# Moving loads, queue entries and three bias additions in a one-launch decoder layer: three phases in one program on one core

## What is computed

```
x = layernorm(x + attn(x))            # 16 heads, "quantum" scores; softmax of s/s
x = layernorm(x + xattn(x, ctx))      # two softmaxes per head, gain 0.3, norm per head, output matmul
x = layernorm(x + ffn(x))             # router picks 2 of 4 experts per token

# ffn, per token, with weights rw of the two chosen experts
e0 = silu(x @ sw_w1) * (x @ sw_w3) @ sw_w2
e1 = gelu(sym @ me_c1w + b) @ me_c2w + me_c2b
e2 = layernorm(h2 + ff) @ ce_gen_w + ce_gen_b
e3 = gelu(x @ ml_w1 + b) @ ml_w2 + ml_b2
out = sum over the chosen experts of rw * e
```

## Time and profile before

| | |
|---|---|
| median of 3 runs | 1595.86 us (1591.67 to 1597.58) |
| profiled execution, its time / its span | 1598.66 us / 1596.9 us |
| busy: PE, PEld, DVE, ACT, POOL | 95%, 68%, 72%, 53%, 23% |
| chain that ended last | PE 86%, DVE 6%, ACT 2%, issue 2%, SPq 2%, DMA 1% |
| mean granted TensorE clock | 0.97 of full |
| transfers issued by SP | 95.41 MB in all; ST 256 x 96 KB, KT 128 x 192 KB, QT 128 x 96 KB |

### The profile page before, as it was taken

The page is one execution under the profiler, slowest core; times in us unless marked ns, Lnnn a source line. Parts: engine busy times, 40 slices in busy tenths (PEclk is TensorE's granted clock), DMA queues, the critical chain, the costliest instruction groups (busy, mean ns, idle before and its releaser), DMA issues.

```text
span 1596.9 us, 28806 instructions
## 1 busy us (share of the span) xinstructions
PE 1523.8 (95%) x11272; PEld 1079.7 (68%) x11272; DVE 1141.8 (72%) x2311; ACT 847.4 (53%) x1121; POOL 367.8 (23%) x399
## 2 busy tenths in 40 slices
PE   6999999888799999999999899999999999999998
PEld 3334333334466666666657788898989888888887
DVE  5445555456699999999964787767676777777675
ACT  4888889763588888888873232222222122222221
POOL 0000100121446666666451320000000000000000
PEclk9999999886799999999998999999999999999999
DMA  7755556355467575665652100000000000000000
GB/s 144 137 108 109 109 109 135 60 87 96 62 95 112 76 111 92 103 96 81 100 166 67 47 14 1 14 1 14 1 14 1 14 1 14 1 1 14 1 14 14
DMA packets 61574, 97.23 MB, mean 61 GB/s; under 512 B 12588, under 2 KB 29880, under 8 KB 61440
## 3 DMA queue, kind: packets, MB, share of 16 engines
q1 hardware_dynamic: 61440, 95.41, 32.9%
HBM read 26.16 MB, written 4.19 MB: 19 GB/s over the span
## 4 chain that ended last, share of the span: by engine, by line
PE 86%; DVE 6%; ACT 2%; issue 2%; SPq 2%; DMA 1%; POOL 0%; POOLq 0%; DVEq 0%; ACTq 0%
PE ps L109 82%; PE ps L1128 2%; SPq L119 2%; ACT PX L1282 1%; ACT H L536 1%; DVE EE L658 1%; PE ps L1090 1%; PE ps L1136 1%; DVE XC L1937 1%; DVE NM L1337 0%; PE ps L1745 0%; PE ps L1060 0%; DMA TA<-TX 0%; PE ps L1736 0%; DVE XH L571 0%
## 5 line engine op out<-in xcount | busy, mean ns | idle before, releaser
L1337 DVE TENSOR_REDUCE NM<-ps 128x4 f32<-128x1024 f32 x256 | 307.8, 1221 | 46.5 <-PE ps L109 45.1
L1282 ACT ACTIVATE PX<-ps 128x1024 f32<-128x1024 f32 x256 | 262.4, 1025 | 82.0 <-PE ps L109 81.0
L536 ACT ACTIVATE H<-ps,b1c 128x1024 f32<-128x1024 f32 x256 | 268.6, 1118 | 43.4 <-PE ps L109 41.8
L1897 ACT ACTIVATE GF<-ps,cols 128x512 f32<-128x512 f32 x128 | 88.2, 689 | 300.9 <-PE ps L109 300.8
L109 PE MATMUL ps<-XC,W_sw_w 128*128 128x512 f32 x768 | 187.3, 395 | 0.0
L2088 DVE CAST GH<-GF 128x512 fp32r<-128x512 f32 x192 | 82.1, 428 | 112.1 <-ACT GF L1897 107.1
L109 PEld LDWEIGHTS ps<-XC,W_sw_w 128*128 128x128 f32 x768 | 141.6, 190 | 28.3
L2196 POOL TENSOR_SCALAR RSc<-AGc 128x4 f32<-128x4 f32 x23 | 6.9, 301 | 607.5 <-DVE AGc L1983 607.5
L109 PE MATMUL ps<-PX,VT 128*32 128x256 f32 x2048 | 141.4, 395 | 1.6 <-DVE X L583 1.5
L1892 ACT ACTIVATE GF<-ps 128x512 f32<-128x512 f32 x64 | 38.2, 597 | 189.0 <-PE ps L109 189.0
L109 PE MATMUL ps<-KT,QT 48*128 48x512 f32 x512 | 132.8, 518 | 5.4 <-DVE NM L1337 3.0
(11 more groups left out here) (233 smaller groups left out, 2567.9 us busy)
## 6 DMA issues: line engine op xcount, KB each, us to landing
ST<-QS SPq DMA_DIRECT2D x256, 96.0 KB, 2.8
KT<-KS SPq DMA_DIRECT2D x128, 192.0 KB, 4.7
QT<-XSb SPq DMA_DIRECT2D x128, 96.0 KB, 4.1
XT<-in_xT_dram SPq DMA_DIRECT2D x8, 512.0 KB, 4.0
raw_a<-in_x_dram SPq DMA_DIRECT2D x8, 512.0 KB, 4.3
CR<-in_ctxT_dram SPq DMA_DIRECT2D x8, 512.0 KB, 5.8
out_dram<-X SPq DMA_DIRECT2D x7, 512.0 KB, 3.0
R_sw_w<-in_sw_w_dram SPq DMA_DIRECT2D x6, 512.0 KB, 5.4
```

The lines of the kernel that those rows point to most:

```text
L536: e.activation(H1[s % 8][:, :, :], PP[s % 3][:, :, :], ACT.Tanh, bias=b1c[:, half:half + 1], scale=1.0).then_inc(act_th, 1)
L1282: e.activation(PX[s % 3][:, :, :, :], PP[2][:, :, :].rearrange("p g (c q) -> p g c q", c=2), ACT.Exp, bias=0.0, scale=0.25).then_inc(act_e ...
L1337: e.tensor_reduce(NM[u % 2][:, qc, :, :, i], PP[qc][:, :, :].rearrange("p g (m k) -> p g m k", m=2), AX.X, ALU.max, negate=True).then_inc( ...
L1897: e.activation(g[:, :], o, f, bias=cols[:, col:col + 1], scale=1.0).then_inc(act_g, 1)
```

## The change

1. SP's `first()` is cut in three and called at J = 25 (CR), 33 (bd) and 41 (wor, kones), not at J = 50.
2. In a step, `put_maxima` comes ahead of `load_ctx`.
3. The eight query transfers of block 0 are issued by ScalarE, two a step in steps -17 to -14, on the same semaphores. SP keeps the key transfers, and no longer waits for the queries' source there.
4. In pair 0 the biases move from i = 17 (all three) to i = 19 (the first) and i = 21 (the other two), behind the second expert of i = 18; the counts that are waited for follow.

```diff
+EARLY_LOADS = (25, 33, 41)
...
-            if J == 50:
+            if J in EARLY_LOADS:
                 for c in range(2):
                     stacked(w, 1, c)
-                first()
+                first(EARLY_LOADS.index(J))
...
-            w.wait_ge(pool_xs, 3 * B + 3)
...
-                dma(e, f32(q[64 * g:64 * g + 48, i, :, :]).rearrange("r b t -> r (b t)"), f32(XS[16 * h:16 * h + 16, c, :, :]), d_ld[B % 2][i])
+                if B:
+                    w.wait_ge(pool_xs, 3 * B + 3)
+                    dma(e, f32(q[64 * g:64 * g + 48, i, :, :]).rearrange("r b t -> r (b t)"), f32(XS[16 * h:16 * h + 16, c, :, :]), d_ld[B % 2][i])
...
-        def first():
-            load_ctx(0)
-            dma(e, bd[:, :, :, :], a["bdw"], d_w)
-            dma(e, wor[:, :, :], a["xwoT"].rearrange("(c p) n -> p c n", c=2), d_w)
-            dma(e, kones[:, :], a["kones"], d_ones)
+        def first(i):
+            if i == 0:
+                load_ctx(0)
+            elif i == 1:
+                dma(e, bd[:, :, :, :], a["bdw"], d_w)
+            else:
+                dma(e, wor[:, :, :], a["xwoT"].rearrange("(c p) n -> p c n", c=2), d_w)
+                dma(e, kones[:, :], a["kones"], d_ones)
 
         def step(s):
+            u = due(s, -4, 8, NU)
+            if u is not None:
+                put_maxima(u)
             p = due(s, -36, 32, NP - 1)
             if p is not None:
                 load_ctx(p + 1)
-            u = due(s, -4, 8, NU)
-            if u is not None:
-                put_maxima(u)
...
+        def first_queries(i):
+
+            after_stack(w, 14)
+            w.wait_ge(dve_w, 4)
+            w.wait_ge(pe_g, 1)
+            w.wait_ge(pool_xs, 3)
+            for g in range(2):
+                h = 2 * i + g
+                dma(e, f32(QT[0][64 * g:64 * g + 48, i, :, :]).rearrange("r b t -> r (b t)"), f32(XS[16 * h:16 * h + 16, 0, :, :]), d_ld[0][i])
+
         def step(s):
+            i = due(s, -17, 1, 4)
+            if i is not None:
+                first_queries(i)
...
-FIRST_BIASES = {17: (1, 2, 3)}
+FIRST_BIASES = {19: (1,), 21: (2, 3)}
...
+def second_added(j):
+
+    return 16 if j else 4
...
-                        w.wait_ge(dve_add, ADDS * j + 2 * u + {"sw": -2, "ce": 2, "ml": 18}[x])
+                        w.wait_ge(dve_add, ADDS * j + 2 * u + {"sw": -2, "ce": 2, "ml": second_added(j) + 2}[x])
...
-            w.wait_ge(dve_add, ADDS * j + 4 * k)
+            w.wait_ge(dve_add, ADDS * j + 4 * k + (0 if j else 4))
...
-                add_expert(j, 1, 24 * j + 15, ADDS * j + 16)
+                add_expert(j, 1, 24 * j + 15, ADDS * j + second_added(j))
```

## The result

The changed kernel takes 1587.38 us in the median of ten runs (1586.24 to 1591.26), where the kernel before took 1594.96 in the same session (ten runs, 1591.67 to 1598.40): a ratio of 0.9956, 95% interval 0.9943 to 0.9969, about 7 us. A later session gave 0.9961, 0.9945 to 0.9976. The profiled execution after has a span of 1588.5 us, 8.4 less than the one before.

What follows compares the result with a forecast made beforehand. TensorE's list of instructions was taken to bound the kernel. Terms 3.9 + 0 + 0 + 5.2 = 9.1 us off the profiled 1598.66 gave 1589.6, less 2.8 for the median: 1586.8 us, range 1579.5 to 1592.5.

Steps and rivals of the forecast that it cites:

- The term of the biases: Pair 0 of phase C, third expert's first output matmul: wait down to 0.3 us at most, 5.25 us back, at least 3.8.
- the term of the loads: Pair 5's `attend`: without the burst at J = 50, TA lands before TensorE comes for it; 3.9 us gained.
- the lower bound is the idle time alone, 1.5 us: Pair 5's `attend`: the least that spreading the loads gives back, TensorE's idle time for TA, 1.5 us.
- The early loads: Pairs 2 and 3: loads ahead of WS don't hold VectorE; no cost taken, 4.6 us at the far end.
- Rival 5: Pair 5: spreading does nothing, since TA stands behind ST and raw_a; 5.2 us gained in all, 1590.7 us; chance 0.05.
- Queries: Passage from phase A to B: maxima start 2 to 3 us late, no seventh wait; 0, from 2.5 gained to 4 lost.
- there the transfers are the limit, not the list: Passage, 339 to 348 us: DMA engines 92% busy at 132 GB/s, so transfers, not SP's list, set the pace.
- a part of the engines seems full: Passage, 351 to 357 us: engines 60% busy at 81 GB/s, yet a query's issue behind the ones takes 2.25 us.
- Maxima ahead of the context: Step -4, ahead of the first scores: maxima level with VectorE's reductions; 0 to 0.6 us gained, taken as 0.
- Nothing came up at i = 21: Pair 0 of phase C: GH(22) 1.5 us late behind the biases, covered by over 1.5 us; without cover, 1.5 us cost.

Runs made afterwards that it cites:

- x9_burst_51: The kernel before with its four second-phase loads together at J = 51 instead of J = 50, right ahead of TA's transfer: 1600.98 us, ratio 1.0044.
- b_again: The kernel before once more, unchanged, for another profiled execution: 1595.77 us, ratio 1.0004.
- x5_ones_late: The changed kernel with both transfers of the rows of ones at the second one's step, -6: 1586.93 us, ratio to the kernel before 0.9949.
- y12: The kernel before with the biases' edit and both transfers of the rows of ones at step -6: 1585.12 us, ratio 0.9937.
- x7: The changed kernel with the first queries back on SP and both transfers of the rows of ones at step -6: 1585.28 us, ratio to before 0.9942.

## Why the prediction was right, and where its steps were not

The forecast was 1586.8 us and the measurement 1587.4. The term of the biases was right; the term of the loads was not, so that the sum came out partly by luck.

**Loads: -3.9, measured -0.2 (-2.1 to +1.8) in the median.** The step that failed: "I take 3.9, since the low clock came right behind that gap", with "the lower bound is the idle time alone, 1.5 us". Both took the one profiled wait as the kernel's own. The mechanism was right (the burst delays TA, and such a wait brings the clock down: x9_burst_51 shows it), but where the burst stood, a margin of some 5 us covered it in all profiled executions but the first. The bound should have been 0. The early loads cost nothing, as forecast: VectorE's reciprocals of pairs 2 and 3 start at 160.63 and 199.74 with no wait for WS, 0.17 us later than before, as the rest of the timeline there.

**From the profiled execution to the median.** The sum was made against 1598.66 and then moved down by the 2.8 us that this execution stood above the median. But the late TA was in the profiled execution and not in the usual one, and is most of what set the two apart (3.4 of 4.4 us against b_again): its gain was counted in the sum and can't be had in the median. Taken out, the forecast would have been 1594.96 - 5.25 = 1589.7, 1 to 2.3 us above what the two sessions gave. What the kernel gained beyond that has no shown cause and is within the uncertainty (see what stays open); it brought the measurement to the forecast, and that was luck. Rival 5 had the loads giving nothing (5.2 us in all, 1590.7), by another reason, that the burst isn't what TA stands behind. The reason was wrong, since TA lands about 2 us later with the burst; the price was nearer to what the loads did than my own term.

**Queries: 0, measured -0.6 us (-2.6 to +1.4) alone, and 0.4 us of gain in the passage.** The size held, and the place of the new wait too: 1.98 to 3.08 us at the first maxima, nothing at the seventh. The way there did not: I let ScalarE issue from 348.24, behind its last tanh, and it issued from 340.54, ahead of it. What made them late then was the two transfers of ones that SP had issued before: with these moved (x5_ones_late) and the keys still ahead, the queries land 2.7 to 4.1 us after their issue, where it was up to 7.0, and nothing waits. And "there the transfers are the limit, not the list" was half of it: the list was lengthened by the ones, and the transfers behind them ran at half the rate (65 against 128 GB/s). The sentence that "a part of the engines seems full" pointed there, and I didn't price it.

**Maxima ahead of the context: 0**, and 0 it was. The first scores came behind a VectorE reduction, as before.

**Biases: -5.25, measured -4.9 (-7.0 to -2.9) alone, 5.25 on the timeline.** Right in size and mechanism: idle time 3.77 and the stretch at the lower clock behind it, both in every execution without the edit. Nothing came up at i = 21.

**What stays open.** The whole change gives 6.2 to 7.0 us. Its parts, by the ratios, give 0.2 (loads), 4.9 (biases), 0.6 (queries) and 0.8 (the order), together 6.5, each uncertain by about 2 us. Whether the loads give 1 us through fewer late TA, or nothing, isn't settled; y12 and x7, which differ in the loads and the order, are 0.2 us apart in their medians, though in two sessions. The place of the low stretches between 385 and 450 us, which moved executions by 1 to 3 us against each other, was not brought to a cause.

The best kernel of the study is y12_biases_ones, 1585.12 us, with only the biases' edit and a pair of numbers for the ones: 0.6% below the kernel before, and in its session 3.5 us below the median of the changed kernel. x7, at 1585.28 us, can't be told from it.

## What to carry to other kernels

A wait in one profiled execution is one draw. Before its price goes into a forecast, ask how much margin its transfer has in like places (here 5.3 us for a landing of 2 to 4), or profile the kernel a second time; and if an execution is above the median, don't subtract both the wait and the difference. A wait for another engine's fixed list of work, like the one for VectorE here, repeated to a hundredth of a microsecond (3.76 or 3.77 us in six executions) and could be counted in full. In a crowded queue look for the small transfers with few rows first: moving two of 64 KB took some 3 us out of the passage, giving eight of 96 KB to another engine 0.4.

## What the hardware showed that was not expected

ScalarE issued transfers while activations that stand ahead of them in its list were still to run: the first query at 340.54, activations to 342.99. Its issues take 0.61 to 2.79 us, in the range of SP's, and the long ones come behind the two transfers of ones that SP had issued at 337.65. In all four executions in which ScalarE issues the queries behind the ones its longest issue is 2.1 to 2.8 us; in x5_ones_late, with the ones moved, it is 0.68. So one engine's transfers lengthened another engine's issues. And the transfers of ones, put together at the end in y12_biases_ones, take 6.58 us to issue four of them.
